# Attention's opening on one Trainium2 core: norm steps one sequence ahead, gathers issued tile by tile

## The chip, the cores and the metric

The kernel runs on one core of one Trainium2 chip. The metric is the device time of one execution in microseconds (us). The time before is the median of three runs, 1563.5 us (1558.94 to 1567.2).

## The reference

Two macaron layers over x of 8 sequences x 512 tokens x 128 features, all fp32. Six parts follow each other, each with a residual addition: a mixture of 8 experts of which the best 2 count (phase "moe0"), attention ("attn"), the same mixture again, a mixture of 16 small experts, a state-space layer, and that mixture again. The change lies in the attention alone:

```python
def _L0_attn_ref(x, Wq, bq, Wk, bk, Wv, bv, Wl, bl, Wo, bo):   # x = layernorm of the residual
    q = (x @ Wq + bq).reshape(b, t, H, hd).transpose(0, 2, 1, 3)              # 16 heads of 8
    k = ((x @ Wk + bk) @ Wl + bl).reshape(b, t, H, lhd).transpose(0, 2, 1, 3)
    v = ((x @ Wv + bv) @ Wl + bl).reshape(b, t, H, lhd).transpose(0, 2, 1, 3)
    attn = softmax(einsum('bhqd,bhkd->bhqk', q, k) / sqrt(hd), axis=-1)
    return einsum('bhqk,bhkd->bhqd', attn, v).transpose(0, 2, 1, 3).reshape(b, t, L) @ Wo + bo
```

## The kernel before

The program is six phases in a row. Each engine has one queue of instructions, written out by hand and executed in order; semaphores join the queues. The residual x stays in SBUF (x_res). A sequence is 4 tiles of 128 tokens.

The attention phase has an opening (functions with the ending _a) and a main part (_b), each with a loop over the 8 sequences b. The opening of one sequence, by engine:

- **PE** (pe_a): three projections of the normalized and transposed sequence xnT (L1670: q, the first of k, the first of v; a 128x512 fp32 matmul is two passes), then the second projection of k (L1676) and of v (L1679), which wait for the biased copies kk_sb and vv_sb. From sequence 3 on, matmuls of the main part of sequence 0 are put in early at three places ("slots" 0, 1, 2): max_pe (L1929), whose scores DVE reduces to row maxima (max_dve, L1935). EARLY says how many: 4 at sequence 3, then 6, 8, 8, 6. Each max_pe waits until DVE has read the one before the last. Then the transposes of the next sequence's xn into bank 7 (norm_pe, L226); mT_pe (L1953) uses bank 7 too.
- **ACT** (act_a): the biased copies kk_sb, vv_sb, q_sb, k_sb (L1702), the first bf16 parts of q and k (q1_act L1732, k1_act L1737), the next sequence's normalization xn (xn_a, L1695, four activations), the copy of the transposed xn to xnT (norm_act, L232), and the second part of k (k2_act, L1741).
- **DVE** (dve_a): the last part of k of the sequence before (split_k2), the statistics of the next sequence (norm_a: L199, L204, results in mv), v with its bias (L1766), the parts of q (L1723 to L1726), split_k1 (L1745), combine (L304, eight instructions), which adds the mixture's gathered rows of sequence b+2 to x_res, and the early maxima.
- **POOL** (pool_a): shift_a (L1789, L186, L188, L1792), which makes shift and rs_y for xn_a from mv, and the gathers (gather, L279): eight indirect DMAs a sequence, two a tile, which fetch the two expert rows of each token from DRAM into one of two buffers staged. The gather of sequence b+3 waits until combine of sequence b+1 has read that buffer. combine(b+2) waits for all eight.
- **SP** (sp_a): stores the three parts of q and of k to DRAM (L1817), counted by saved, and for sequences 0 to 3 loads the parts of sequences 0 and 1 back in another arrangement (L1840, L1842; 24 DMAs each time).

parts has two buffers for q and two for k, picked by par = b % 2. q1_act and k1_act wait for saved of all stores up to sequence b-1.

Of the kernel before, what the change touches and what calls it, by code (L numbers as in the profile page):

```python
# [15 lines left out]
B, T, E = 8, 512, 128  # L16
TILES = T // P
# [43 lines left out]
def build(nc, a, out, phases=PHASES):  # L61
    nc.disable_value_cache = True
    with ExitStack() as ctx:
# [3 lines left out]
        def sem(name):  # L67
            return ctx.enter_context(nc.semaphore(name))
# [152 lines left out]
        def norm_pe(f):  # L221

            need(nc.tensor, xn_ready, f + 1)
            need(nc.tensor, xnT_ready, f)
            for i in range(TILES):
                last = nc.tensor.transpose(bank[7][:, i * P:(i + 1) * P], xn[:, i, :], ident[:])  # L226
            last.then_inc(xnT_ps, 1)
# [1381 lines left out]
        def attn_phase(n):  # L1609
# [3 lines left out]
            f0 = base(n)  # L1613
# [3 lines left out]
                     "m_split", "mT_ps", "mT_sb", "st_ready", "exp_done", "av_done", "o_sb", "oT_ps", "o_tok", "o_chain",  # L1617
                     "otT_ps", "ot_sb", "z_ready", "x_bo")
            s = {k: sem(f"p{n}_{k}") for k in names}
            saved = {c: sem(f"p{n}_{c}_saved") for c in "qk"}  # L1620
            ld = [[sem(f"p{n}_qk_loaded{i}{g}") for g in range(H // HG)] for i in range(2)]
            m_ld = [[sem(f"p{n}_m_loaded{i}{g}") for g in range(H // HG)] for i in range(2)]
            new_phase()
# [35 lines left out]
            def parts_due(b):  # L1659

                upto = [sum(sum(EARLY.get(k, ())) for k in range(x)) // (HG * TILES // 2) for x in (b - 1, b)]
                return range(*upto)

            def pe_a(b, par, first_, last_):
                x = xnT[par][:]
                nc.tensor.wait_ge(xnT_ready, f0 + b + 1)
                for to, w, ps, free, per in ((Q_BANK, wq_p[:], "q_ps", "q_sb", 2), (K_BANK, wk[:], "kk_ps", "k_sb", 1),
                                             (V_BANK, wv[:], "vv_ps", "v_sb", 1)):
                    need(nc.tensor, s[free], per * b)
                    nc.tensor.matmul(bank[to][:], w, x, start=True, stop=True).then_inc(s[ps], 1)  # L1670
                for g in parts_due(b):
                    mT_pe(0, g)
                for m in early(b, 0):
                    max_pe(0, m)
                nc.tensor.wait_ge(s["kk_sb"], b + 1)
                nc.tensor.matmul(bank[K_BANK][:], wl_p[:], kk_sb[:], start=True, stop=True).then_inc(s["k_ps"], 1)  # L1676
                nc.tensor.wait_ge(s["vv_sb"], b + 1)
                for i in range(TILES):
                    last = nc.tensor.matmul(bank[V_BANK][:, i * P:(i + 1) * P], vv_sb[:, i * P:(i + 1) * P], wl[:], start=True, stop=True)  # L1679
                last.then_inc(s["v_ps"], 1)  # L1680
                for m in early(b, 1):
                    max_pe(0, m)
                if not last_:
                    for g in parts_due(b):
                        nc.tensor.wait_ge(s["mT_sb"], g + 1)
                    norm_pe(f0 + b + 1)
                for m in early(b, 2):
                    max_pe(0, m)

# [8 lines left out]
            def act_a(b, par, first_, last_):  # L1698
                def biased(i, ps, dst, at, done, free, count):
                    nc.scalar.wait_ge(s[ps], b + 1)  # L1700
                    need(nc.scalar, s[free], count)
                    nc.scalar.activation(dst[:], bank[i][:], ACT.Identity, bias=vecs[:, at:at + 1]).then_inc(s[done], 1)  # L1702
                biased(K_BANK, "kk_ps", kk_sb, V_BK, "kk_sb", "k_ps", b)
                biased(V_BANK, "vv_ps", vv_sb, V_BV, "vv_sb", "v_ps", b)
                biased(Q_BANK, "q_ps", q_sb, V_BQ, "q_sb", "q_split", b)
                q1_act(b, par)
                biased(K_BANK, "k_ps", k_sb, V_BL, "k_sb", "k_split", b)
                k1_act(b, par)
                if not last_:
                    xn_a(f0 + b + 1, b + 1)  # L1710
                for g in parts_due(b):
                    mT_act(0, 0, g)
                if not last_:
                    norm_act(f0 + b + 1, 1 - par)
                k2_act(b, par)

            def split_q(v, b, par):
# [10 lines left out]

            def q1_act(b, par):
                nc.scalar.wait_ge(s["q_sb"], 2 * b + 1)  # L1730
                need(nc.scalar, saved["q"], 16 * b)
                nc.scalar.copy(parts["q"][par][:, 0, :], q_sb[:]).then_inc(s["q_sb"], 1)  # L1732

            def k1_act(b, par):
                nc.scalar.wait_ge(s["k_sb"], b + 1)
                need(nc.scalar, saved["k"], 16 * b)
                nc.scalar.copy(parts["k"][par][:, 0, :], k_sb[:]).then_inc(s["k1"], 1)  # L1737

            def k2_act(b, par):
# [19 lines left out]
            def dve_a(v, b, par, first_, last_):  # L1759
                if not first_:  # L1760
                    split_k2(v, b - 1, 1 - par)
                if not last_ and not first_:
                    norm_a(v, f0 + b + 1, b + 1)
                early_dve(v, b, 0)
                v.wait_ge(s["v_ps"], b + 1)
                nc.vector.tensor_tensor(  # L1766
                    v_all[:, bass.ds(b * TILES, TILES), :, 0:HD], bank[V_BANK][:].rearrange("p (i h d) -> p i h d", i=TILES, d=HD),
                    bl_bc[:].rearrange("p (h d) -> p h d", d=HD).unsqueeze(1).to_broadcast([P, TILES, H, HD]),
                    ALU.add).then_inc(s["v_sb"], 1)
                if last_:  # L1770
                    v.wait_ge(s["v_sb"], B)
                    nc.vector.memset(bank[6][:], 0.0).then_inc(s["zeroed"], 1)
                early_dve(v, b, 1)
                need(v, s["q_split"], b)
                split_q(v, b, par)
                split_k1(v, b, par)
                if 2 < b + 2 < B:
                    combine(v, occ0, b + 2)
                early_dve(v, b, 2)
                if last_:  # L1780
                    split_k2(v, b, par)
                if first_:
                    nc.vector.memset(v_all[:, :, :, HD:], 1.0).then_inc(s["zeroed"], 1)
                    nc.vector.memset(ones3, 1.0).then_inc(s["zeroed"], 1)

            def shift_a(f):
# [4 lines left out]
                nc.gpsimd.wait_ge(rs_ready, f + 1)  # L1791
                nc.gpsimd.tensor_tensor(shift[:], shift[:], rs_y[:], ALU.mult).then_inc(shift_ready, 1)  # L1792

            def pool_a(b, par, first_, last_):
                if first_:
                    shift_a(f0 + b + 1)
                    stored_by(nc.gpsimd, occ0, b + 3)
                    gather(nc.gpsimd, occ0, b + 3)
                    y_wait(nc.gpsimd, occ0)
                    return  # L1800
                if b + 3 < B:
                    gather(nc.gpsimd, occ0, b + 3, FIRST_HALF)
                if not last_:
                    shift_a(f0 + b + 1)
                if b + 3 < B:
                    gather(nc.gpsimd, occ0, b + 3, SECOND_HALF)

            NLD = 12
            M0, M1 = 6 * HD, 6 * HD + 3
# [4 lines left out]
            def sp_a(b, par, first_, last_):  # L1814
                for c in "qk":
                    nc.sync.wait_ge(s[c + "_split"], b + 1)
                    nc.sync.dma_start(scratch[c][b:b + 1].rearrange("o j p t -> p (o j) t"), parts[c][par][:]).then_inc(saved[c], 16)  # L1817
                if b == 1:
                    nc.sync.wait_ge(s["zeroed"], 2)
                    for m in ka:  # L1820
                        for f in (0, HALF):
                            nc.sync.dma_start(m[f + M0:f + M1, :, :], ones3.unsqueeze(1).to_broadcast([3, H // 2, T])).then_inc(s["qk_ones"], 16)
                for g in parts_due(b):
                    m_sp(0, 0, g)
                if b < 4:
                    for c in "qk":
                        nc.sync.wait_ge(saved[c], 16 if b < 2 else 32)
                    for g in range(b % 2 * 2, b % 2 * 2 + 2):
                        load(b // 2, b // 2, g)

# [300 lines left out]
            def sp_b(b, par, first_, last_):  # L2131
                m_sp(b, par, GB - 1)
                if last_:
                    return
                for g in range(GB):


                    nc.sync.wait_ge(s["st_ready"], PER * b + GP * (g + 1))
                    if b + 2 < B:
                        for c in "qk":  # L2140
                            nc.sync.wait_ge(saved[c], 16 * (b + 3))
                        load(b + 2, par, g)
                    if g < GB - 1:
                        m_sp(b + 1, 1 - par, g)
# [636 lines left out]
```

## Time and profile before

| | |
|---|---|
| median of three runs | 1563.5 us |
| the profiled execution's own time | 1577.35 us |
| its span | 1575.6 us |
| mean granted TensorE clock | 0.94 of full |
| busy share of the span: PE, DVE, ACT, POOL | 83%, 75%, 58%, 28% |
| opening of the attention, first projection to first matmul of the main part | 288.70 to 407.77 us |
| first biased copy of k (L1702) of sequences 1 to 7 starts at | 306.63, 317.30, 332.37, 350.00, 363.28, 382.89, 399.29 us |

An engine's busy share is a mean over six unlike phases; the opening is 119 us of the span. Times below are microseconds from the start of the span.

### The profile page before, as it was taken

The numbers are of one execution on the slowest core, as the hardware profiler recorded it, in microseconds if no ns is written. First come the engines' busy times: TensorE is split into PE (matmuls) and PEld (weight loads), VectorE is DVE, ScalarE is ACT, GpSimd is POOL, SyncE is SP. The second block draws the span as 40 slices with busy tenths as digits, with TensorE's granted clock in tenths as the row PEclk, the third lists the DMA queues.
The fourth block names the chain that finished last, engine by engine and source line by source line (L and its number), as shares of the span: only waits on it lengthen the run. The fifth ranks groups of instructions, "written<-read, shape, count | busy, mean of one in ns | idle before, by whom it ended". The sixth has DMA issues, their size and how long they took to land.

```text
span 1575.6 us, 20686 instructions
## 1 busy us (share of the span) xinstructions
PE 1313.8 (83%) x6518; PEld 782.7 (50%) x6518; DVE 1188.9 (75%) x2583; ACT 909.5 (58%) x1439; POOL 438.6 (28%) x577
## 2 busy tenths in 40 slices
PE   3488999655788888888867989978999878879998
PEld 3367787322122222222235878755666444556665
DVE  5567898569799999999436799976877663668875
ACT  4377676434477877776855867633334366534342
POOL 6662336561000000121234233622341120201000
PEclk9999999877699999998988999989999998989999
DMA  8141363242111111110033122234454011054344
GB/s 286 47 138 54 110 238 94 85 144 68 51 32 34 38 34 32 45 45 19 12 116 148 54 68 80 75 94 104 100 129 98 11 31 32 1 109 90 74 108 108
DMA packets 83113, 127.66 MB, mean 81 GB/s; under 512 B 17332, under 2 KB 37268, under 8 KB 81980
## 3 DMA queue, kind: packets, MB, share of 16 engines
q1 hardware_dynamic: 75836, 111.64, 25.5%
q0 software_dynamic: 7168, 14.69, 3.2%
q8 instruction: 53, 0.87, 0.2%
q14 instruction: 56, 0.46, 0.1%
HBM read 82.23 MB, written 41.16 MB: 78 GB/s over the span
## 4 chain that ended last, share of the span: by engine, by line
PE 57%; DVE 21%; ACT 8%; issue 7%; SPq 4%; DMA 1%; another core or an unknown queue 1%; POOL 1%; DVEq 0%; ACTq 0%; POOLq 0%
PE bank L1419 6%; PE bank L1995 6%; PE pair L809 5%; PE pair L807 5%; PE pair L808 5%; DVE shared L1935 5%; PE pair L1335 4%; PE pair L1337 4%; PE pair L1336 4%; ACT shared L1985 3%; PE pair L1977 3%; PE pair L1929 3%; DVE shared L863 2%; PE bank L879 1%
## 5 line engine op out<-in xcount | busy, mean ns | idle before, releaser
L1935 DVE TENSOR_REDUCE shared<-pair 128x2 f32<-128x1024 f32 x256 | 305.2, 1219 | 30.9 <-PE pair L1929 25.3
L1985 ACT ACTIVATE shared<-pair 128x1024 f32<-128x1024 f32 x256 | 258.5, 1023 | 77.4 <-PE pair L1977 75.3
L863 DVE TENSOR_TENSOR shared<-shared 128x512 fp32r<-128x512 f32 x232 | 195.7, 851 | 80.2 <-ACT shared L853 50.2
L807 PE MATMUL pair<-shared 128*128 128x512 f32 x464 | 197.4, 425 | 11.6 <-issue 6.2
L1386 ACT ACTIVATE shared<-pair 128x512 f32<-128x512 f32 x144 | 85.7, 595 | 185.0 <-PE pair L1337 179.9
L808 PE MATMUL pair<-shared 128*128 128x512 f32 x464 | 187.2, 403 | 0.0
L809 PE MATMUL pair<-shared 128*128 128x512 f32 x464 | 187.0, 403 | 0.0
L1335 PE MATMUL pair<-shared 128*128 128x512 f32 x288 | 156.7, 544 | 6.2 <-DVE shared L1369 6.0
L848 ACT ACTIVATE shared<-pair,shared 128x512 f32<-128x512 f32 x168 | 115.9, 690 | 65.4 <-PE pair L809 59.6
L590 POOL DMA_INDIRECT xs_rows<-shared,slots x112 | 115.0, 1027 | 133.3 <-ACT shared L1985 63.4
L1995 PE MATMUL bank<-shared 128*9 128x512 f32 x1024 | 141.3, 625 | 10.2 <-ACT shared L1985 10.2
L1398 DVE TENSOR_TENSOR shared<-shared,pair 128x512 f32<-128x512 f32 x128 | 87.0, 682 | 64.4 <-ACT shared L1386 59.2
L1929 PE MATMUL pair<-shared 48*128 48x512 bf16 x512 | 102.2, 402 | 33.0 <-DVE shared L1935 16.6
L279 POOL DMA_INDIRECT staged<-ys_rows,slots x112 | 117.2, 1047 | 43.4 <-issue 29.4
L1419 PE MATMUL bank<-shared,down_w 128*128 128x512 f32 x256 | 128.5, 593 | 0.6 <-DVE shared L1407 0.6
L1977 PE MATMUL pair<-shared 51*128 51x512 bf16 x512 | 103.0, 402 | 29.9 <-DVE shared L1935 28.2
L1337 PE MATMUL pair<-shared 128*128 128x512 f32 x288 | 115.9, 402 | 0.0
L1336 PE MATMUL pair<-shared 128*128 128x512 f32 x288 | 115.5, 401 | 0.0
L1977 PEld LDWEIGHTS pair<-shared 51*128 51x128 bf16 x512 | 24.9, 94 | 173.7 <-issue 84.2
L807 PEld LDWEIGHTS pair<-shared 128*128 128x128 f32 x464 | 90.9, 196 | 30.5 <-issue 11.9
L809 PEld LDWEIGHTS pair<-shared 128*128 128x128 f32 x464 | 90.2, 194 | 21.3
L808 PEld LDWEIGHTS pair<-shared 128*128 128x128 f32 x464 | 90.9, 196 | 16.2
(341 smaller groups left out, 2288.6 us busy)
## 6 DMA issues: line engine op xcount, KB each, us to landing
shared<-p_coef_rows SPq DMA_DIRECT2D x64, 512.0 KB
shared<-xs_rows SPq DMA_DIRECT2D x42, 256.0 KB, 2.7
ys_rows<-shared SPq DMA_DIRECT2D x42, 256.0 KB
w_keep<-shared SPq DMA_DIRECT2D x8, 1024.0 KB
shared<-w_keep SPq DMA_DIRECT2D x16, 512.0 KB
xs_rows<-shared SPq DMA_DIRECT2D x1, 5376.0 KB, 18.2
p_q_parts<-shared SPq DMA_DIRECT2D x8, 384.0 KB
p_k_parts<-shared SPq DMA_DIRECT2D x8, 384.0 KB
```

Source lines behind the costliest of these rows:

```text
L807: nc.tensor.matmul(out_bank, w_hi, x_hi, start=start, stop=False)
L808: nc.tensor.matmul(out_bank, w_hi, x_lo, start=False, stop=False)
L809: return nc.tensor.matmul(out_bank, w_lo, x_hi, start=False, stop=stop)
L863: nc.vector.tensor_tensor(hl[u % RING][:], hid[u % RING][:], hh[u % RING][:], ALU.subtract).then_inc(s["dve_done"], 1)
L1335: nc.tensor.matmul(out_bank, w_hi, x_hi, start=start, stop=False)
L1336: nc.tensor.matmul(out_bank, w_hi, x_lo, start=False, stop=False)
L1337: return nc.tensor.matmul(out_bank, w_lo, x_hi, start=False, stop=stop)
L1419: nc.tensor.matmul(bank[6][:], w, h, start=(j == 0), stop=(j == IT - 1)).then_inc(s["down_done"], 1)
L1935: nc.vector.tensor_reduce(mneg[:, i, 2 * c:2 * c + 2], pair_of("max", b, m)[:], AX_X, ALU.max, negate=True).then_inc(s["mx_read"], 1)
L1977: last = nc.tensor.matmul(pair_of("exp", b, 2 * st + p)[:, f, :], ka[par][rows, c, kt * P:(kt + 1) * P], qa[par][rows, c, :], start=True, ...
L1985: nc.scalar.activation(probs[st % 2][:, 2 * p:2 * p + 2, :], pair_of("exp", b, 2 * st + p)[:], ACT.Exp, scale=scale).then_inc(s["exp_done" ...
L1995: last = nc.tensor.matmul(bank[6][32 * hh:32 * hh + HD + 1, :], v_all[:, b * TILES + kt, hh % 2 * (H // 2) + g * HG // 2 + hh // 2, :], pr ...
```

## The change

Four things change, all in the opening.

1. norm_a(b+2) moves to the end of DVE's sequence b, behind combine(b+2); before, norm_a(b+1) stood at the start of sequence b. shift_a(b+2) follows in pool_a(b). On ACT, xn_a(b+1) moves to the front of sequence b and norm_act(b+1) to behind vv_sb. On PE, norm_pe(b+1) moves from the end of sequence b to right behind the three projections.
2. The gathers of sequence b+3 are issued tile by tile, each tile behind a count of ACT's: tile 0 behind kk_sb of sequence b, tile 1 behind q1_act of b, tiles 2 and 3 behind kk_sb and vv_sb of sequence b+1. shift_a(b+2) stands between tiles 1 and 2.
3. saved is counted by buffer: q1_act and k1_act of b wait only for the store of sequence b-2.
4. mT_pe moves behind the second slot of early maxima.

```diff
 def pe_a
-                for g in parts_due(b):
-                    mT_pe(0, g)
+                if not last_:
+                    if b and parts_due(b - 1):
+                        nc.tensor.wait_ge(s["mT_sb"], parts_due(b - 1)[-1] + 1)
+                    norm_pe(f0 + b + 1)
                 for m in early(b, 0):
                     max_pe(0, m)
...
-                if not last_:
-                    for g in parts_due(b):
-                        nc.tensor.wait_ge(s["mT_sb"], g + 1)
-                    norm_pe(f0 + b + 1)
+                for g in parts_due(b):
+                    nc.tensor.wait_ge(xnT_ready, f0 + min(b + 2, B))
+                    mT_pe(0, g)
 def act_a
+                if not last_:
+                    xn_a(f0 + b + 1, b + 1)
                 biased(K_BANK, "kk_ps", kk_sb, V_BK, "kk_sb", "k_ps", b)
                 biased(V_BANK, "vv_ps", vv_sb, V_BV, "vv_sb", "v_ps", b)
+                if not last_:
+                    norm_act(f0 + b + 1, 1 - par)
...
-                if not last_:
-                    xn_a(f0 + b + 1, b + 1)
                 for g in parts_due(b):
                     mT_act(0, 0, g)
-                if not last_:
-                    norm_act(f0 + b + 1, 1 - par)
                 k2_act(b, par)
 def q1_act (k1_act likewise)
-                need(nc.scalar, saved["q"], 16 * b)
+                need(nc.scalar, saved["q"][par], 16 * (b // 2))
 def dve_a
-                if not last_ and not first_:
-                    norm_a(v, f0 + b + 1, b + 1)
...
                 if 2 < b + 2 < B:
                     combine(v, occ0, b + 2)
+                if b + 2 < B:
+                    norm_a(v, f0 + b + 2, b + 2)
                 early_dve(v, b, 2)
+            def spaced(name, count):
+                nc.gpsimd.wait_ge(s[name], count)
+
             def pool_a(b, par, first_, last_):
                 if first_:
-                    shift_a(f0 + b + 1)
-                    stored_by(nc.gpsimd, occ0, b + 3)
-                    gather(nc.gpsimd, occ0, b + 3)
-                    y_wait(nc.gpsimd, occ0)
-                    return
-                if b + 3 < B:
-                    gather(nc.gpsimd, occ0, b + 3, FIRST_HALF)
-                if not last_:
-                    shift_a(f0 + b + 1)
-                if b + 3 < B:
-                    gather(nc.gpsimd, occ0, b + 3, SECOND_HALF)
+                    shift_a(f0 + 1)
+                    stored_by(nc.gpsimd, occ0, 3)
+                for tile in range(TILES if b + 3 < B else 0):
+                    if tile < 2:
+                        spaced(*(("kk_sb", b + 1), ("q_sb", 2 * b + 2))[tile])
+                    else:
+                        spaced(*(("kk_sb", b + 2), ("vv_sb", b + 2))[tile - 2])
+                    gather(nc.gpsimd, occ0, b + 3, (tile, tile + 1))
+                    if tile == 1:
+                        shift_a(f0 + b + 2)
+                    if first_ and tile == 0:
+                        y_wait(nc.gpsimd, occ0)
+                if b + 3 >= B and b + 2 < B:
+                    shift_a(f0 + b + 2)
```

## Rows read from the trace of the kernel before

**Rows 1.** Waits of the opening (288 to 405 us): total, times, longest.

```profile
POOL shift L1789 <- DVE mv L204: 27.9, 3, 15.4
ACT shared L1732 <- DMA p_q_parts<-shared: 12.5, 4, 6.3
```

**Rows 2.** Timeline of ACT: start, duration, line; kk_sb of sequences 1 and 4, one xn_a.

```profile
306.63 0.69 ACT L1702 ACTIVATE shared<-pair,vecs 128x512 f32<-128x512 f32 x1 [3.49 <-PE pair L1670]
...
343.23 1.64 ACT L1695 ACTIVATE xn<-x_res,shift,rs_y 128x128 f32<-128x128 f32 x4
...
350.00 0.69 ACT L1702 ACTIVATE shared<-pair,vecs 128x512 f32<-128x512 f32 x1 [2.82 <-issue]
```

**Rows 3.** Timeline of PE in the opening.

```profile
326.76 1.12 PE L226 MATMUL bank<-ident,xn 128*128 128x128 f32 x4 [5.99 <-ACT xn L1695]
...
379.07 2.07 PE L1670 MATMUL pair<-xnT,wq_p 128*128 128x512 f32 x2
...
386.34 1.12 PE L1676 MATMUL pair<-shared,wl_p 128*128 128x512 f32 x2
387.31 1.05 PE L1679 MATMUL bank<-w_l,shared 128*128 128x128 f32 x8
...
407.77 0.61 PE L1977 MATMUL pair<-shared 51*128 51x512 bf16 x2
```

**Rows 4.** Timeline of DVE in the opening.

```profile
296.38 0.69 DVE L1766 TENSOR_TENSOR shared<-bank,bl_bc 128x512 f32<-128x512 f32 x1 [7.74 <-issue]
...
303.78 0.86 DVE L199 BATCH_NORM_STATS2 stats<-x_res 128x6 f32<-128x128 f32 x4
...
310.75 0.68 DVE L1723 TENSOR_TENSOR shared<-shared 128x512 f32<-128x512 f32 x1
...
312.54 0.69 DVE L1745 TENSOR_TENSOR shared<-shared 128x512 f32<-128x512 f32 x1
313.14 2.31 DVE L304 SCALAR_TENSOR_TENSOR x_res<-staged,w_tok,x_res 128x128 f32<-128x128 f32 x8
315.48 0.69 DVE L1749 TENSOR_TENSOR shared<-shared 128x512 bf16<-128x512 f32 x1
...
377.25 1.22 DVE L1935 TENSOR_REDUCE shared<-pair 128x2 f32<-128x1024 f32 x1
...
384.74 3.49 DVE L1935 TENSOR_REDUCE shared<-pair 128x2 f32<-128x1024 f32 x3 [1.29 <-PE pair L1929]
```

**Rows 5.** Timeline of POOL: gathers and shift_a.

```profile
284.92 1.12 POOL L279 DMA_INDIRECT staged<-ys_rows,slots  x1 [0.43 <-issue]
...
295.08 0.94 POOL L279 DMA_INDIRECT staged<-ys_rows,slots  x1 [0.31 <-issue]
...
305.23 0.25 POOL L1789 TENSOR_SCALAR shift<-mv 128x4 f32<-128x4 f32 x1 [4.95 <-DVE mv L204]
...
307.34 1.12 POOL L279 DMA_INDIRECT staged<-ys_rows,slots  x1 [0.16 <-issue]
...
315.72 1.27 POOL L279 DMA_INDIRECT staged<-ys_rows,slots  x1 [3.48 <-DVE x_res L304]
```

**Rows 6.** Timeline of POOL: the last indirect scatter of the first mixture.

```profile
115.71 1.11 POOL L590 DMA_INDIRECT xs_rows<-shared,slots  x1 [3.35 <-PE pair L809]
```

**Rows 7.** Timeline of SP: the load that waits for that scatter; a store of k.

```profile
118.19 3.48 SPq L1205 DMA_DIRECT2D shared<-xs_rows  x3
...
338.10 0.48 SPq L1817 DMA_DIRECT2D p_k_parts<-shared  x1
```

**Rows 8.** Timeline of ACT: what waits for that store of k.

```profile
342.71 0.62 ACT L1737 CAST shared<-shared 128x512 bf16<-128x512 f32 x1 [0.74 <-DMA p_k_parts<-shared]
```

**Rows 9.** Windows behind the opening: busy by engine (instructions), granted clock, DMA share, GB/s.

```profile
418.00:426.00 8.00, 7.47 (x34) 0.93 (x32) 4.90 (x4) 3.88 (x4) 0.00 (x0) 0.50 0.01 2
426.00:434.00 8.00, 7.65 (x46) 1.83 (x42) 6.01 (x9) 5.69 (x7) 0.00 (x0) 0.67 0.19 50
434.00:442.00 8.00, 6.79 (x52) 1.42 (x50) 7.47 (x12) 5.70 (x8) 0.00 (x0) 1.00 0.06 17
```

More of the change, by code:

```diff
@@ L1619, in attn_phase @@
             s = {k: sem(f"p{n}_{k}") for k in names}
-            saved = {c: sem(f"p{n}_{c}_saved") for c in "qk"}
+            saved = {c: [sem(f"p{n}_{c}_saved{i}") for i in range(2)] for c in "qk"}
             ld = [[sem(f"p{n}_qk_loaded{i}{g}") for g in range(H // HG)] for i in range(2)]
@@ L1735, in k1_act @@
                 nc.scalar.wait_ge(s["k_sb"], b + 1)
-                need(nc.scalar, saved["k"], 16 * b)
+                need(nc.scalar, saved["k"][par], 16 * (b // 2))
                 nc.scalar.copy(parts["k"][par][:, 0, :], k_sb[:]).then_inc(s["k1"], 1)
@@ L1816, in sp_a @@
                     nc.sync.wait_ge(s[c + "_split"], b + 1)
-                    nc.sync.dma_start(scratch[c][b:b + 1].rearrange("o j p t -> p (o j) t"), parts[c][par][:]).then_inc(saved[c], 16)
+                    nc.sync.dma_start(scratch[c][b:b + 1].rearrange("o j p t -> p (o j) t"), parts[c][par][:]).then_inc(saved[c][par], 16)
                 if b == 1:
@@ L1826, in sp_a @@
                     for c in "qk":
-                        nc.sync.wait_ge(saved[c], 16 if b < 2 else 32)
+                        nc.sync.wait_ge(saved[c][b // 2], 16)
                     for g in range(b % 2 * 2, b % 2 * 2 + 2):
@@ L2140, in sp_b @@
                         for c in "qk":
-                            nc.sync.wait_ge(saved[c], 16 * (b + 3))
+                            nc.sync.wait_ge(saved[c][par], 16 * ((b + 2) // 2 + 1))
                         load(b + 2, par, g)
```

## The prediction

> **What bounds the kernel now.** I first read the page for where the opening lies, then the list of waits of the opening, then the timeline of each engine through it, and last the windows behind it. The waits name what the change is after: ACT's first part of q stands still 12.5 us in four places for a store of the sequence before [rows 1], because stores queue on SP behind 24 loads. One such store is issued at 338.10 and ACT goes on at 342.71 [rows 7, 8]. The 27.9 us that POOL waits for the statistics [rows 1] cost nothing before: they are made early in the same sequence and xn_a comes late in it. The timelines show three regimes. In sequences 1 to 3 ACT, PE and the store wait set the pace: kk_sb starts at 306.63 for sequence 1 and at 350.00 for sequence 4 [rows 2], 43.4 us for three rounds, 14.5 each. In sequences 4 to 6 DVE, with early maxima of about 1.17 us each [rows 4], is nearly always busy. At the end the projections of sequence 7 hold it, and the main part starts at 407.77 [rows 3]. All that follows moves with that instant.
>
> **The change part by part.** I call X the end of the xn step on ACT at the front of a round, and follow the new queues from one X to the next.
>
> *Counting stores by buffer.* It removes the 12.5 us of stalls: the store of two sequences earlier has long landed. Nothing new queues on SP, and its loads keep their order.
>
> *The norm step on the main path.* Nothing is added in work; what changes is who waits. Before, the statistics of b+1 were made at the start of sequence b, so POOL and xn had most of a round. Now norm_a(b+2) ends DVE's chain of round b, and xn_a(b+2) stands on ACT ahead of the biased copies of round b+1; behind it wait KK, V, Q, K and both parts, and on PE norm_pe waits ahead of the second projections. So the two engines can't start the round before DVE and POOL have ended the last one. The loop, without early maxima:
> - norm_pe at X+0.05, 1.1 (a four-transpose group took 1.12) [rows 3]; second k and v projections 0.97 and 1.05 [rows 3]: v is in PSUM, and L1766 starts, at X+3.25. KK is ready at X+0.6.
> - L1766 takes a 0.6 slot of DVE; L1723 to L1745 1.8 (310.75 to 312.54), L1745 0.6 [rows 4]: X+6.25.
> - combine 2.35 (313.14 to 315.48) [rows 4]: X+8.6. Statistics to POOL's start 1.45 (303.78 to 305.23) [rows 4, 5]: X+10.05.
> - shift_a 2.0 (305.23 to 307.2; the next gather starts at 307.34) [rows 5], then xn_a 1.65 [rows 2] with a hop of 0.1: the loop closes at 13.75.
>
> *The gathers.* Eight took 284.92 to 295.08, 10.15 us, so four take 5.05 [rows 5]. Before, they lay over 12 us ahead of their combine and cost nothing. Now tiles 2 and 3 of sequence b+2 may start only behind kk_sb of round b, at X+0.85, and are issued by X+5.9. Their landing isn't shown in the trace, as no combine waits for one. The nearest row is an indirect DMA of the same 128 rows in the other direction: the last scatter ends at 116.8 and SP's waiting load starts at 118.19 [rows 6, 7], 1.4 us on quiet queues. The upper bound is the store of k beside loads, from the end of its issue at 338.6 to 342.7, 4.1 us [rows 7, 8]. In rounds 1 to 3 SP's loads run beside the gathers, so I take 2.4, a little under the middle because the size is that of the scatter. combine then starts at X+8.3 and not at X+6.25: the loop is 15.8. Were the landing 1.4, the chain would give 14.8; POOL gives the same as a floor, since it issues all eight gathers (X+0.85 to X+11.0) ahead of shift_a 2.0, hop and xn 1.75. With 4.1 the loop is 17.5.
>
> The Trainium skill ("DMA: Bandwidth & Descriptors", Anatomy of one DMA) gives a DMA issued from GpSimd a fixed cost of about 2.0 us, most of it the receipt of the write at its target. The rows bracket that (1.4 and 4.1); by it the two rounds below would each be 0.4 shorter and the sum +6.8.
>
> *Round by round.* X of round 1: in round 0 the transposes of norm_pe stand between the projections and the second ones, and push L1766 from 296.38 [rows 4] to 296.95; then 3.0 of split, 1.45 statistics and hop, 2.0, 1.75 give X1 = 305.1. kk_sb of round 1 then starts at 305.1, 1.5 earlier than at 306.63 [rows 2]. Rounds 1 and 2 at 15.8: X3 = 336.7. Round 3 has three early maxima ahead of combine: first slot at X+1.6, then 2.35, 0.6, 1.15, 1.8, 0.6, combine 2.35, statistics 1.45, 2.0, 1.75: 15.7, the gathers just hidden. X4 = 352.4; before, kk_sb of round 4 began at 350.00 [rows 2], so the lead is gone and 2.4 lost. Round 4 has four maxima ahead and a split of the maxima of 0.8: 17.5, X5 = 369.9. DVE's own work in it is 15.1; the rest is the shift, xn and norm_pe hole. In round 5, five maxima, the longer slot 0 and combine put the statistics ready at X+14.5 and maximum 15 read at X+15.8. The next matmul, the projections of sequence 6 and the first maximum behind them follow: from the end of maximum 15 (377.25+1.22 = 378.47) to the maximum at 384.74 it took 6.3 [rows 4], projections from 379.07 [rows 3]. Now norm_pe lies in there and mT_pe doesn't: 7.0. That maximum starts at 392.7, against 384.74: 8.0 late. Rounds 6 and 7 have neither combine nor norm in either kernel and follow as before; mT_pe moved behind the slots gives 0.3 back. **Sum: +7.7 us** at 407.77 [rows 3].
>
> The profiled execution's own time was 1577.35 at a span of 1575.6, 1.75 outside; +7.7 makes it 1585.05. It ran 13.9 above the median of the runs. The change is a difference of schedule, so I put it on the median: 1563.5 + 7.7 = 1571.2.
>
> **Rivals.**
> *The landing is slow* (one in eight). Gathers and loads share the DMA engines. With 4.1, rounds 1 and 2 are 1.7 longer each and round 3 1.7: +7.7+5.1 = +12.8, 1576. For it: k's store took 4.1 in just such a stretch. Against: it is six times as large as one gather. The Trainium skill ("GPSIMD Engine Reference", Specifications) says that GpSimd shares its SBUF interfaces with VectorE and contends with instructions of two SBUF inputs; combine and the splits are such, which speaks against gathers paced into them.
>
> *The floor* (two in ten). The landing hides fully and only POOL's order binds: rounds 1 and 2 at 14.8: +5.7, 1569.
>
> *The stalls outweigh the loop* (one in eight, near no change). If the full clock holds in rounds 1 to 3, norm_pe and the second projections shrink by half, 1.5 a round; with splits hidden as well and POOL's gathers less than 10 us, rounds of 13.2 cancel the loss. From there down the change wins. Against: POOL's floor of 14.8 doesn't depend on PE.
>
> *The clock returns early* (one in eight; the other side). In the before trace PE is at the half clock up to about 431 us, 23.5 us into the main part, where 8 us hold 34 matmuls against 52 at the full one [rows 9]; a round of 16 takes 3.8 us against 2.5, so six rounds cost 7.8 us. The projections of sequences 6 and 7, some 5.3 us at the half clock (379.07 on [rows 3]), would save 2.6 each. If packed matmuls bring the full clock by 392 and it stays, 7.7-7.8-5.2 = -5.3: 1558. It decides from the point where the clock comes 20 us sooner. Against: PE still idles about 6 us in every round.
>
> **How the numbers follow.** The forecast (loop bound by gather landing, +6.5 to +11) has 0.43, the slow landing 0.12, the floor 0.20, the cancelling 0.12, the clock 0.13. The predicted time is 1571. About 0.5%, 7.8 us, is what a measurement of this kernel can tell from no change. +7.7 lies on it: half of the forecast's case (0.22), all of the slow landing (0.12), and a little of the floor, where the clock falls worse than before (0.06), are beyond it: slower 0.40. Faster by over 0.5% is most of the clock case, with the floor under it or with more early maxima gaining than I see: 0.12. The rest, 0.48, is within. The range takes in the clock case and the slow landing with a little over: 1558 to 1579.
>
> **What the changed profile would show.** No wait of L1732 or L1737 for a store. L1695 waits for POOL at the front of each round, and kk_sb starts right at its end, at about 305, 321, 337, 352, 370. POOL's idle before gathers is ended by ACT's L1702 in place of DVE. If combine's start follows the last gather's end by less than 2 us with DVE idle before it, the landing term is right; if it follows L1745 at once, the floor holds. DVE shows a hole of about 2 us at the start of rounds 4 and 5. The first main matmul comes at about 415. I am wrong if the rounds of sequences 1 to 3 are under 14 us, which would mean that shift_a runs ahead of its gathers or that xn_a finds its input ready.

## The result, and the profile after

| | before | after |
|---|---|---|
| median of the runs of this comparison | 1561.22 us (4 runs, 1556.98 to 1567.2) | 1577.89 us (4 runs) |
| ratio, with its 95% interval | | 1.009 (1.005 to 1.013) |
| the profiled execution: own time, span | 1577.35, 1575.6 us | 1573.59, 1571.9 us |
| the opening: first projection to first matmul of the main part | 288.70 to 407.77: 119.07 us | 276.61 to 406.80: 130.19 us |
| from there to the end of the span | 1167.8 us | 1165.1 us |

One of the four executions of the kernel after took 3092.71 us; the median takes it in, the ratio leaves it out. The other three took 1573.01, 1573.59 and 1582.2 us.

The change makes the kernel slower by 0.9%, 14 us (8 to 20). Two more kernels with this queue order, below, came out at 1.0078 and 1.0059. The two profiled executions alone would say the opposite, 1573.59 against 1577.35. The reason lies ahead of the change: this opening begins 12.1 us earlier than that of before, in code that the diff doesn't touch. Over all the profiles below its start wanders from 276 to 300 us. So I read the opening by its own length. That is 11.1 us longer, and it repeats well: three kernels with this queue order have 130.2, 130.7 and 130.3 us.

The diff moves the line numbers: in the kernel after xn_a is L1696, a biased copy L1703, q1_act L1733, k1_act L1738, the end of shift_a L1793, the second projections of k and v L1678 and L1681, v with its bias L1765, an early maximum L1937 on PE and L1943 on DVE. In the kernels of the experiments they differ by a few lines again.

Waits of the opening after, read from 288 to 415 us (total, times, longest). The whole opening, 276.6 to 406.8, gives the same figures, except that POOL's line has 22.8 us in six:

```profile
PE bank L226 <- ACT xn L1696: 36.9, 5, 9.4
ACT xn L1696 <- POOL shift L1793: 30.2, 6, 6.5
...
POOL staged L279 <- ACT shared L1703: 12.8, 5, 2.7
...
DVE x_res L304 <- DMA staged<-ys_rows,slots: 1.3, 2, 1.0
```

Against [rows 1], ACT's stall for a store is gone (12.5 us). ACT now stands 30.2 us for POOL at the front of six rounds, and PE behind it for ACT, up to 9.4 us at a time. The loop through four engines is there; it can be followed on their timelines. ACT first:

```profile
290.40 1.65 ACT L1696 ACTIVATE xn<-x_res,shift,rs_y 128x128 f32<-128x128 f32 x4 [2.83 <-POOL shift L1793]
291.96 0.67 ACT L1703 ACTIVATE shared<-pair,vecs 128x512 f32<-128x512 f32 x1
...
306.11 1.65 ACT L1696 ACTIVATE xn<-x_res,shift,rs_y 128x128 f32<-128x128 f32 x4 [5.71 <-POOL shift L1793]
...
322.23 1.65 ACT L1696 ACTIVATE xn<-x_res,shift,rs_y 128x128 f32<-128x128 f32 x4 [6.48 <-POOL shift L1793]
...
339.17 1.65 ACT L1696 ACTIVATE xn<-x_res,shift,rs_y 128x128 f32<-128x128 f32 x4 [5.04 <-POOL shift L1793]
...
358.10 1.65 ACT L1696 ACTIVATE xn<-x_res,shift,rs_y 128x128 f32<-128x128 f32 x4 [5.04 <-POOL shift L1793]
```

From one of these to the next is a round: 15.71, 16.12, 16.94 and 18.93 us for sequences 1 to 4. PE in the rounds of sequences 2 and 4, and its second projections in a late one:

```profile
307.81 1.12 PE L226 MATMUL bank<-ident,xn 128*128 128x128 f32 x4 [7.98 <-ACT xn L1696]
308.72 1.91 PE L1678 MATMUL pair<-shared,wl_p 128*128 128x512 f32 x2
310.42 1.53 PE L1681 MATMUL bank<-w_l,shared 128*128 128x128 f32 x8
...
342.88 2.08 PE L1678 MATMUL pair<-shared,wl_p 128*128 128x512 f32 x2
344.75 1.44 PE L1681 MATMUL bank<-w_l,shared 128*128 128x128 f32 x8
...
385.42 1.12 PE L1678 MATMUL pair<-shared,wl_p 128*128 128x512 f32 x2
386.38 1.05 PE L1681 MATMUL bank<-w_l,shared 128*128 128x128 f32 x8
```

Behind an idle time of 8 us the second projections take 1.91 and 1.53 us; the same instructions without such a hole ahead take 1.12 and 1.05. The granted clock (the third number from the end) is the half one over the start of the round of sequence 4:

```profile
340.87:344.87 4.00, 4.00 (x11) 1.80 (x12) 2.30 (x2) 2.89 (x5) 2.59 (x3) 0.50 0.33 89
```

DVE and POOL close the loop:

```profile
296.67 0.69 DVE L1765 TENSOR_TENSOR shared<-bank,bl_bc 128x512 f32<-128x512 f32 x1 [6.52 <-PE bank L1681]
...
300.01 2.31 DVE L304 SCALAR_TENSOR_TENSOR x_res<-staged,w_tok,x_res 128x128 f32<-128x128 f32 x8 [0.26 <-DMA staged<-ys_rows,slots]
...
316.12 2.32 DVE L304 SCALAR_TENSOR_TENSOR x_res<-staged,w_tok,x_res 128x128 f32<-128x128 f32 x8 [1.02 <-DMA staged<-ys_rows,slots]
...
319.45 0.38 DVE L204 BATCH_NORM_AGGREGATE mv<-stats 128x2 f32<-128x6 f32 x4
```

POOL in the same rounds:

```profile
296.83 0.94 POOL L279 DMA_INDIRECT staged<-ys_rows,slots  x1 [0.30 <-issue]
...
308.61 1.11 POOL L279 DMA_INDIRECT staged<-ys_rows,slots  x1 [2.54 <-ACT shared L1703]
...
312.53 0.94 POOL L279 DMA_INDIRECT staged<-ys_rows,slots  x1 [0.30 <-issue]
...
319.93 0.57 POOL L1790 TENSOR_SCALAR shift<-mv 128x4 f32<-128x4 f32 x1 [1.38 <-DVE mv L204]
```

The last of the four gathers that combine needs ends its issue at 313.47 (312.53+0.94), and combine, which had nothing else to wait for, starts at 316.12: 2.65 us. In the round before it is 297.77 to 300.01: 2.24 us.

Behind the opening, windows as in [rows 9]:

```profile
418.00:426.00 8.00, 6.52 (x50) 1.44 (x50) 7.23 (x11) 5.60 (x8) 0.00 (x0) 1.00 0.07 21
426.00:434.00 8.00, 7.10 (x53) 1.73 (x52) 7.56 (x9) 6.09 (x7) 0.00 (x0) 1.00 0.13 32
```

The clock is back some 14 us sooner than in [rows 9], and the rest of the span is 2.7 us shorter. The first experiment and its repeat show below that the clock's return isn't the change's doing, and what it is worth.

### The profile page after: what moved, and what is told of

It reads as the page before. It is cut to its first block, busy times and chain, and to the rows that moved or that the text cites. A ratio compares the mean times of both kernels' runs of the same rounds, so it can differ in the third digit from the quotient of the medians.

```text
span 1571.9 us, 20707 instructions
## 1 busy us (share of the span) xinstructions
PE 1312.4 (83%) x6518; PEld 784.1 (50%) x6518; DVE 1188.7 (76%) x2583; ACT 910.5 (58%) x1439; POOL 442.9 (28%) x577
## 4 chain that ended last, share of the span: by engine, by line
PE 57%; DVE 21%; ACT 8%; issue 6%; DMA 3%; SPq 2%; POOL 2%; DVEq 0%; POOLq 0%; ACTq 0%
PE bank L2003 6%; PE bank L1419 6%; PE pair L807 6%; PE pair L808 5%; PE pair L809 5%; DVE shared L1943 5%; PE pair L1335 3%; PE pair L1337 3%; PE pair L1336 3%; ACT shared L1993 3%; PE pair L1937 3%; PE pair L1985 3%; DVE x_res L304 2%; PE bank L879 2%; DVE shared L863 1%
## 5 line engine op out<-in xcount | busy, mean ns | idle before, releaser
L1943 DVE TENSOR_REDUCE shared<-pair 128x2 f32<-128x1024 f32 x256 | 305.3, 1219 | 39.6 <-PE pair L1937 37.2
L807 PE MATMUL pair<-shared 128*128 128x512 f32 x464 | 198.5, 428 | 11.1 <-issue 6.4
L590 POOL DMA_INDIRECT xs_rows<-shared,slots x112 | 119.7, 1069 | 125.3 <-ACT shared L1993 69.4
L1937 PE MATMUL pair<-shared 48*128 48x512 bf16 x512 | 103.0, 405 | 40.4 <-DVE shared L1943 22.4
```

The source lines that it names most:

```text
L807: nc.tensor.matmul(out_bank, w_hi, x_hi, start=start, stop=False)
L1943: nc.vector.tensor_reduce(mneg[:, i, 2 * c:2 * c + 2], pair_of("max", b, m)[:], AX_X, ALU.max, negate=True).then_inc(s["mx_read"], 1)
```

## The experiments

Openings are from the first projection to the first main matmul of the profiled execution; ratios are against the kernel before, on the same chip.

**Only the store counts (part 3 alone), on the kernel before.**

```diff
-            saved = {c: sem(f"p{n}_{c}_saved") for c in "qk"}
+            saved = {c: [sem(f"p{n}_{c}_saved{i}") for i in range(2)] for c in "qk"}
...
-                need(nc.scalar, saved["q"], 16 * b)
+                need(nc.scalar, saved["q"][par], 16 * (b // 2))
...
-                need(nc.scalar, saved["k"], 16 * b)
+                need(nc.scalar, saved["k"][par], 16 * (b // 2))
```

> The kernel before with part 3 alone (stores counted by buffer). Loop theory: the stalls of ACT for a store, 12.5 us before, go, and nothing takes their place, since the norm step keeps its order: the rounds of sequences 2 and 3 shorten by about 3 and 5 us, later rounds stay bound by DVE; opening 119 -> about 111 us, time about 8 us (0.5%) below the kernel before. Rival, the stalls cover another wait that comes last (gathers or POOL): opening within 2 us of before, no change. Second rival, that part 3 itself is what slows the changed kernel: slower here too.

Opening 113.8 us, 5.3 shorter. ACT's first parts follow their copies at once; here in the round of sequence 3, where L1732 had stood 6.27 us before:

```profile
332.84 0.68 ACT L1702 ACTIVATE shared<-pair,vecs 128x512 f32<-128x512 f32 x1
333.55 0.62 ACT L1732 CAST shared<-shared 128x512 bf16<-128x512 f32 x1
334.08 0.68 ACT L1702 ACTIVATE shared<-pair,vecs 128x512 f32<-128x512 f32 x1
334.79 0.62 ACT L1737 CAST shared<-shared 128x512 bf16<-128x512 f32 x1
```

Of 12.5 us of stalls 5.3 were on the path; I hadn't split that figure. From one xn_a to the next, rounds 2 and 3 shortened by 1.7 and 5.5 us as expected, and rounds 4 to 6 took 2.8 of it back. The ratio was 1.0017 (0.9976 to 1.0058).

**The change, its gathers unpaced.**

```diff
             def spaced(name, count):
-                nc.gpsimd.wait_ge(s[name], count)
+                pass
```

> The changed kernel without the waits for ACT's counts ahead of the gathers. Loop theory: the round is DVE's chain, shift_a, xn_a, KK; the gathers' landing added only 0.3 and 1.0 us of wait ahead of combine in rounds 1 and 2, so the opening shortens by 1 to 2 us (130 -> about 128.5), time about 1.009 of before less 0.001. Rival, the pacing of the gathers makes the loss: opening 120 to 123 us, time back at before's.

Opening 130.7, ratio 1.0078 (1.0036 to 1.012): neither my 128.5 nor the rival's 120 to 123. POOL now has the gathers issued early and waits 2.88 us for the statistics:

```profile
313.50 1.02 POOL L279 DMA_INDIRECT staged<-ys_rows,slots  x1 [0.30 <-issue]
317.41 0.57 POOL L1790 TENSOR_SCALAR shift<-mv 128x4 f32<-128x4 f32 x1 [2.88 <-DVE mv L204]
```

Rounds 1 and 2 fell to 15.37 and 15.18 (by 0.34 and 0.94), as the waits of combine said they would. Rounds 3 and 4 grew to 17.75 and 20.54, and what was won was lost again. Two parts of it are seen: in those rounds L1681 took 1.91 and 1.71 us, where it took 1.38 and 1.44 in the same rounds after, and in round 4 DVE stood 1.26 us ahead of a maximum, for which the trace names no releaser. So pacing isn't what costs 11 us in this queue order.

**The change, with a single store count again.**

```diff
-            saved = {c: [sem(f"p{n}_{c}_saved{i}") for i in range(2)] for c in "qk"}
+            saved = {c: sem(f"p{n}_{c}_saved") for c in "qk"}
```

(and its five uses as before)

> The changed kernel with one count of stores for both buffers, as before. Loop theory: the rounds are 16 to 19 us, so the store of the sequence before lands before q1_act asks for it; at most 0.5 us of waiting in round 3, opening 130 to 131 us, time as the changed kernel, about 1.009. Rival, the count by buffer is a gain that works in the changed kernel: some 8 us slower still, 1.014.

Opening 130.3, ratio 1.0059 (1.0013 to 1.0106). (Of this profile only the opening is read; its execution took 1606.39 us, and the rest of its span, 1174.7 us, is the longest of all.) The stalls do not come back at all. Neither L1733 nor L1738 waits for a store in any round, not even in that of sequence 3, where the old order stood 6.27 us:

```profile
348.93 0.69 ACT L1703 ACTIVATE shared<-pair,vecs 128x512 f32<-128x512 f32 x1
349.66 0.62 ACT L1733 CAST shared<-shared 128x512 bf16<-128x512 f32 x1
```

In rounds of 16 us and more the store of the sequence before has landed by then, as expected. What took 5.3 us off the old order takes 0.1 off the new one, because the longer rounds have removed the stalls already.

**The change, with the order of xn_a, norm_act, norm_pe and mT_pe of before.** The statistics stay behind combine, the counts and the pacing stay.

```diff
 def act_a
-                if not last_:
-                    xn_a(f0 + b + 1, b + 1)
                 biased(K_BANK, "kk_ps", kk_sb, V_BK, "kk_sb", "k_ps", b)
...
                 k1_act(b, par)
+                if not last_:
+                    xn_a(f0 + b + 1, b + 1)
...
 def pe_a
-                if not last_:
-                    if b and parts_due(b - 1):
-                        nc.tensor.wait_ge(s["mT_sb"], parts_due(b - 1)[-1] + 1)
-                    norm_pe(f0 + b + 1)
+                for g in parts_due(b):
+                    mT_pe(0, g)
```

> The changed kernel with ACT's and PE's order of before (xn_a and norm_act behind k1_act, norm_pe at the end, mT_pe ahead of the first slot); statistics one ahead, paced gathers and counts by buffer stay. Loop theory: what costs is xn_a at the head of ACT's round, behind POOL; with it back at the end the statistics have 5 to 9 us of room, no store is waited for, and the opening takes about 111 us, the time is about 8 us under before's (0.995). Rival, pacing and statistics behind combine cost by themselves: opening 125 to 130 us, time at 1.005 or above.

Opening 120.8: 9.4 of the 11.1 us come from where these four steps stand. That lies between my 111 and the rival's 125 to 130. Ratio 1.0049 (1.0014 to 1.0085). Now the pacing is seen, on DVE ahead of combine:

```profile
334.01 0.69 DVE L1745 TENSOR_TENSOR shared<-shared 128x512 f32<-128x512 f32 x1
339.04 2.31 DVE L304 SCALAR_TENSOR_TENSOR x_res<-staged,w_tok,x_res 128x128 f32<-128x128 f32 x8 [4.34 <-DMA staged<-ys_rows,slots]
```

**The hole on PE filled.** PE's idle time ahead of norm_pe is filled with matmuls whose result nothing reads; all else is the change. If the half clock behind the hole is what makes a round longer than 15.8, this shortens it.

```diff
                         nc.tensor.wait_ge(s["mT_sb"], parts_due(b - 1)[-1] + 1)
+                    for _ in range({1: 11, 2: 17, 3: 20, 4: 18, 5: 12}.get(b, 0)):
+                        nc.tensor.matmul(bank[7][:, 0:256], wl_p[:], x[:, 0:256], start=True, stop=True)
                     norm_pe(f0 + b + 1)
```

> The changed kernel with 11, 17, 20, 18 and 12 matmuls of 128x256 whose results nobody reads, put on PE ahead of norm_pe in rounds 1 to 5, to fill the 5 to 9 us in which PE waits for xn. If PE's fall to the half clock in that hole is what made my second projections 1.5 us too short, the granted clock stays at 1 through rounds 1 to 5, L1678 to the end of L1681 falls from 3.6 to 2.1 us, rounds 3, 4 and 5 shorten by 1 to 2 us each, rounds 1 and 2 by 0.3 at most (their combine waits for gathers); opening 130.2 -> about 126. Rival, the longer rounds 3 to 5 come from the early maxima and ACT, not from the clock: 129 to 131.

Opening 126.8, 3.4 shorter (one execution, no ratio). Rounds 3, 4 and 5 fell to 14.95, 16.96 and 18.97 us from 16.94, 18.93 and 19.63. PE in round 4, and a window of that stretch with the granted clock (the third number from the end):

```profile
344.82 7.93 PE L1675 MATMUL bank<-xnT,wl_p 128*128 128x256 f32 x36
353.33 0.66 PE L226 MATMUL bank<-ident,xn 128*128 128x128 f32 x4 [0.58 <-ACT xn L1698]
...
354.45 1.13 PE L1680 MATMUL pair<-shared,wl_p 128*128 128x512 f32 x2
355.42 1.05 PE L1683 MATMUL bank<-w_l,shared 128*128 128x128 f32 x8
...
353.33:356.47 3.14, 3.14 (x20) 1.95 (x20) 2.12 (x2) 3.11 (x6) 2.03 (x2) 1.00 0.34 97
```

L1680 and L1683 are the second projections, L1678 and L1681 with 2.08 and 1.44 us in the same round after. The half clock is shown, and with it its price in rounds 3 to 5.

Rounds 1 and 2 grew by 0.7 and 0.5 us, for another reason. The fillers ended 0.5 and 3.3 us ahead of norm_pe, so they held nothing up. In round 1 DVE was then ready early, and combine stood 2.80 us for its gathers (POOL, then DVE):

```profile
310.38 0.94 POOL L279 DMA_INDIRECT staged<-ys_rows,slots  x1 [0.31 <-issue]
...
313.90 2.32 DVE L304 SCALAR_TENSOR_TENSOR x_res<-staged,w_tok,x_res 128x128 f32<-128x128 f32 x8 [2.80 <-DMA staged<-ys_rows,slots]
```

In round 2 it stood 1.86 us and began 2.89 us behind the last gather's issue, though the trace names no releaser there. The half clock and the landing of the gathers are therefore alternatives in these two rounds: whichever ends later sets combine, and the faster matmuls bought nothing.

**The hole filled, and the gathers unpaced.** The two edits above together.

> The same with the gathers unpaced. Loop theory: with neither landing nor half clock, a round is 3.3 + 3.0 + 2.35 + 1.45 + 2.0 + 1.75 = 13.8 us in rounds 1 and 2 and no less, so the opening is about 122 us, still longer than before's 119. Rival, another wait closes the loop (POOL's order, ACT): rounds stay at 15 or more.

Opening 124.3. Rounds 1 to 3 were 13.50, 15.42 and 14.88 us. The first is under what I had called POOL's floor of 14.8; that floor counted gathers that wait for kk_sb, and here they don't. Round 4 took 22.26, with stalls on DVE that the trace puts down to nothing in the core, while PE stood 6.51 us:

```profile
357.76 2.36 DVE L1945 TENSOR_REDUCE shared<-pair 128x2 f32<-128x1024 f32 x2 [3.09 <-issue]
362.83 0.69 DVE L1767 TENSOR_TENSOR shared<-bank,bl_bc 128x512 f32<-128x512 f32 x1 [2.72 <-remote]
365.70 1.22 DVE L1945 TENSOR_REDUCE shared<-pair 128x2 f32<-128x1024 f32 x1 [2.18 <-remote]
```

With this stall in it, the length of this opening says little.

**Order back, and unpaced.** The fourth and the second edit together: the move of the statistics and the counts are left of the change, with tiles 2 and 3 of each sequence's gathers still behind shift_a on POOL.

> ACT's and PE's order of before and unpaced gathers; of the change only the statistics behind combine and the counts by buffer are left. In the run with paced gathers (opening 120.8) combine of round 3 waited 4.3 us for its gathers. If pacing made that, it goes and the opening is 116 to 117; what then still lies above the 113.8 of counts alone is the move of the statistics: before, DVE made them while PE ran the projections, now they stand ahead of the last maxima, for which PE's next projections wait, 1.35 us in each of rounds 4 and 5. Rival, the statistics cost nothing: 113 to 114.

Opening 114.6, ratio 0.9982 (0.9938 to 1.0026). Against 120.8 the pacing costs 6.2 us here; against the counts alone (113.8) the move of the statistics costs 0.8. In that lies a wait of 3.52 us of one combine, whose gathers come behind shift_a.

**The counts and the pacing, on the kernel before.**

```diff
+                for tile in range(TILES if b + 3 < B else 0):
+                    if tile == 2:
+                        shift_a(f0 + b + 2)
+                    nc.gpsimd.wait_ge(s[("kk_sb", "q_sb", "kk_sb", "vv_sb")[tile]], (b + 1, 2 * b + 2, b + 2, b + 2)[tile])
+                    gather(nc.gpsimd, occ0, b + 3, (tile, tile + 1))
```

> The kernel before with counts by buffer and the paced gathers, statistics and the order of ACT and PE as before. Pacing theory: the last gather is issued about 7.3 us behind kk_sb (4 gathers and shift_a) and lands 2.3 later, against a combine that could start 6 us behind kk_sb in round 2 and 9 in round 3: 2 to 4 us of waiting in rounds 1 and 2, opening 116 to 119 against 113.8. Rival, pacing costs nothing where the loop is open: 113 to 114.

Opening 120.2, 6.4 above the counts alone and above my 116 to 119, ratio 0.9996 (0.9948 to 1.0043). Pacing costs the same with the statistics early or late.

**The counts alone, a second time.**

> The kernel of the first experiment once more (before, with counts by buffer alone), since its time (1.0017, 0.9976 to 1.0058) did not resolve the 5.3 us by which its opening is shorter. Expected: opening 113 to 115 again, ratio 0.9966, interval of 0.4% either way. Rival: the main part behind the opening takes back what the opening gives: opening as said, ratio 1.000 or above again.

Opening 113.9, against 113.8. Ratio 0.9934 (0.9899 to 0.997), where the first measurement had 1.0017 (0.9976 to 1.0058): the same kernel, two intervals that don't meet. The two were measured on different chips, each beside the kernel before. So either the gain differs by chip, or these intervals are narrower than the true scatter; then the one of the main comparison may be too. The profiles show one source of scatter outside the opening. Windows of ten microseconds, 10 us behind the first main matmul. The first profile of this kernel:

```profile
413.70:423.70 10.00, 7.54 (x60) 1.64 (x56) 8.76 (x11) 7.43 (x9) 0.00 (x0) 1.00 0.06 21
```

The second profile, of the repeat:

```profile
422.20:432.20 10.00, 9.12 (x40) 1.30 (x36) 6.06 (x5) 5.47 (x6) 0.00 (x0) 0.50 0.01 2
```

60 matmuls at the full clock, or 40 at the half one, of one program. What that costs can be read off one instruction of ACT some 170 us later, in the first profile of the counts, the repeat, the kernel before and the kernel after:

```profile
576.15 0.59 ACT L2002 COPY shared<-bank 128x512 f32<-128x512 f32 x1 [0.66 <-PE bank L1995]
...
588.39 0.58 ACT L2002 COPY shared<-bank 128x512 f32<-128x512 f32 x1 [0.67 <-PE bank L1995]
...
583.99 0.58 ACT L2002 COPY shared<-bank 128x512 f32<-128x512 f32 x1 [0.67 <-PE bank L1995]
...
579.29 0.58 ACT L2010 COPY shared<-bank 128x512 f32<-128x512 f32 x1 [0.67 <-PE bank L2003]
```

It starts 172.45, 176.18, 176.22 and 172.49 us behind the first main matmul (at 403.70, 412.21, 407.77 and 406.80): the late return costs 3.7 us. The rest of the span was 1161.1 and 1170.7 us in the first two, so 5.9 of their 9.6 us arose later still, from a cause that I didn't find. Of the twelve profiles here, eight have the clock back 10 to 15 us behind the first main matmul, and four (before, the repeat of the counts, the two combinations with unpaced gathers) 20 to 25 us behind it. The chip of the first measurement shows both, in different kernels.

**The counts, with PE's waits filled.** Unread matmuls ahead of norm_pe in rounds 0 to 4 and ahead of the last early maximum in rounds 5 and 6, on top of the counts alone.

```diff
+                    for _ in range({0: 5, 1: 6, 2: 9, 3: 6, 4: 6}.get(b, 0)):
+                        nc.tensor.matmul(bank[7][:, 0:256], wl_p[:], x[:, 0:256], start=True, stop=True)
                     norm_pe(f0 + b + 1)
...
+                        for _ in range({5: 11, 6: 6}[b]):
+                            nc.tensor.matmul(bank[Q_BANK][:, 0:256], wl_p[:], x[:, 0:256], start=True, stop=True)
```

> The same with 5, 6, 9, 6 and 6 unread matmuls of 128x256 ahead of norm_pe in rounds 0 to 4, and 11 and 6 ahead of the last early maximum of rounds 5 and 6. If PE's half clock behind each hole is a cost here too, the three projections take 2.9 us and not 5.5, and the rounds bound by PE (1 to 3, and the ends of 5 and 6) shorten by 1.5 to 2.5 us each: opening 104 to 108, ratio 0.992. Rival, DVE's maxima bind from round 4 and the projections hide behind them: 110 to 113; or the fillers come late and delay norm_pe: above 113.

Opening 115.0, ratio 0.9964 (0.9929 to 0.9999): no better than the counts alone, and far from my 104 to 108. A stall without a releaser in the core lies in it, on ACT:

```profile
332.62 1.65 ACT L1701 ACTIVATE xn<-x_res,shift,rs_y 128x128 f32<-128x128 f32 x4 [3.10 <-issue]
339.12 0.58 ACT L232 COPY xnT<-bank 128x512 f32<-128x512 f32 x1 [4.85 <-remote]
```

## Why the prediction was right, and where its sizes were off

The time fell in the range, near its upper end, and the forecast mechanism is the one that ran; the size was too small, +7.7 us where the opening grew by 11.1 and the time by 14 (8 to 20). The single chance that deserved more weight was "slower by over 0.5%".

*The loop: right.* Laid over the opening of before (12.1 us added), kk_sb starts at 304.1, 319.8, 335.9, 352.8 and 371.7, against 305, 321, 337, 352 and 370 as predicted. That its place in the queues is what costs is shown by putting xn_a, norm_act, norm_pe and mT_pe back: 9.4 us.

*The landing: right in size, wrong in weight.* I took 2.4 us; combine starts 2.24 and 2.65 us behind the last gather's issue. The Trainium skill ("DMA: Bandwidth & Descriptors", Anatomy of one DMA) gives such a DMA about 2.0 us fixed; both measured values lie above it, though they leave out the issue itself. (By that figure my sum would have come to +6.9, not to the +6.8 that I wrote.) I let the landing stretch a round of 13.75 to 15.8, by 2.05. Unpaced rounds took 15.4 and 15.2, and the landing added 0.3 and 0.9. So the round was long already, for the reason of the next point, and the landing hid that error: 15.7 and 16.1 came close to 15.8 in part by luck. With the hole filled combine stood 2.80 and 1.86 us for the gathers, so the landing would have counted about as forecast if the second projections had run as I charged them. My sign for it, a combine less than 2 us behind the last gather, was set badly: the term itself was 2.4, and 2.24 and 2.65 came.

*The second projections: the step that failed.* "Second k and v projections 0.97 and 1.05" came from [rows 3], where PE had been at work. The transposes ahead of them I charged at 1.1, from a row behind a hole of 5.99 us, so the sum mixed the two clocks. In rounds 1 to 5 of this loop PE comes out of 5.3 to 9.4 us of waiting, and the two take 1.9 to 2.1 and 1.4 to 1.9. L1765 starts at X+4.6 and X+4.2 in rounds 1 and 2, not X+3.25. There the landing hid most of it. In rounds 3 to 5 nothing does: 16.94 against 15.7, 18.93 against 17.5, and 24.07 against 22.8 from xn in round 5 to the maximum behind the projections of sequence 6, together +3.9 us. Filling the hole gave rounds 3 to 5 back 4.6 us, with the transposes quicker too. The gap of the sum, 3.4 us, is this term less 1.0 that the opening's first part was quicker (X1 15.4 us into the opening, 16.4 predicted), plus 0.5 from the other stretches. The warning was in my own text: the rival of the stalls has these matmuls shrink by half with the full clock, while the sum had charged them at the full one.

*The stores: gone, but not by the counts.* Neither L1733 nor L1738 waits for a store, as forecast. With the single count brought back they don't either, and the opening changes by 0.1 us: here it is the longer rounds that remove the stalls. The counts are worth 5.3 us only while the loop is open.

*The rivals.* The slow landing did not happen. The floor did not bind, but was near: behind its eight gathers POOL still waited 0.59 and 1.38 us for the statistics in rounds 1 and 2, so by my estimate its order alone would have made them 15.1 and 14.7 (15.71 less 0.59, 16.12 less 1.38). The clock came back some 14 us sooner than in the profile of before, but later than the point I gave (392; the projections of sequences 6 and 7 still took 1.91 to 2.08 us each), and one unchanged kernel shows both returns. DVE's holes at the start of rounds 4 and 5 were 3.8 and 2.6 us (about 2 predicted), and POOL's idle ahead of the gathers was ended by ACT, as forecast.

**How the 11.1 us come together**, each from one profile against the last: counts by buffer -5.3 (119.1 to 113.8); statistics behind combine +0.8 (114.6); pacing +6.2 (120.8); the order of ACT and PE, with xn_a and norm_pe at the front, +9.4 (130.2). In another order of edits the parts have other values: with xn_a in front, the pacing is worth 0.5 the other way and the counts 0.1, and without pacing the same order of ACT and PE costs 16.1 (114.6 to 130.7).

*What stays open.* The time grew by 14 us, the opening by 11.1, and the rest of the profiled span shrank by 2.7, of which the clock's earlier return makes 3.7 and later parts take 1.0 back. In the 170 us behind the opening the kernel after runs as the counts alone do, to 0.04 us (172.49 against 172.45), so the change costs nothing there. Further on the scatter between executions is larger than the difference. The interval (8 to 20) holds 11 easily. What makes the clock return late or early, what the stalls without a releaser are, and all of what lengthens the late unpaced rounds, was not found.

**A version with a shorter opening than both** is the counts alone: 113.8 and 113.9 us against 119.1 before and 130.2 after, ratios to the kernel before 1.0017 and 0.9934. Only the second measurement shows a gain over before on the whole kernel; what the openings' -5.3 us would make is 0.9966.

## What to carry to other kernels

Before work is moved ahead in one engine's queue, write down the loop that it closes: the head of a round that waits for the tail of the last one puts every engine's latency in a row, and the longer round can remove a stall elsewhere by itself, so that an edit against that stall gives nothing. Take the durations of matmuls in such a loop from rows behind an idle time of the same length, not from busy stretches. Where two waits meet at one instruction, only the later one counts, and removing it uncovers the other. Where a change sits in 8% of the span and single times wander by 1%, compare the length of that stretch over several profiles, and price each part with and without the others.

## What the runs showed of the hardware

- An indirect gather of 128 rows landed 2.24 and 2.65 us behind the end of its issue in the kernel after, beside loads, and 1.9 to 3.5 us over all the profiles in which combine waited for one. POOL issues one each 1.25 us. The longest gather took 1.63 us, beside a split of DVE in the kernel without pacing; the shortest take 0.94. The Trainium skill ("GPSIMD Engine Reference", Specifications) warns of contention between GpSimd and VectorE; in these rows it can be at most 0.7 us a gather.
- Behind each of five idle times of 5.3 to 9.4 us PE's transposes and the second projection of k ran at the half clock (granted 0.50; 1.9 to 2.1 us against 1.0 to 1.1 for two passes of 128x512). With unread matmuls in the hole the granted clock was 1.00 in rounds 1, 3 and 4, and the projection took 1.12 or 1.13.
- In one kernel the full clock came back 10 us behind the first main matmul in one execution, and over 20 us behind it in another, on another chip. The late return cost 3.7 us.
- Waits with no releaser in the core: about 5 us on several engines in two openings with added matmuls (DVE and PE, ACT and PE), and one of 2.0 to 3.6 us on ACT in six of the seven openings with ACT's old order, before among them (3.11). The added matmuls are thus not their only setting.
